# A two-layer decoder on one core: ternary weight passes moved to ScalarE, 63 expert blocks, the fourth convolution tile without diagonal products

## The reference

```
# layer 0, third block: top-4 of 32 experts
topk_logits, topk_idx = jax.lax.top_k(logits, K)
y = jnp.sum(outs * topk_weight[..., None], axis=1)      # outs: one row per token and chosen expert
# layer 1, first block: a state-space model
xz = jnp.einsum('bld,ed->ble', xn, in_proj_w)
x_inner, z = jnp.split(xz, 2, axis=-1)                  # 512 channels each
xc = conv_general_dilated(xc, conv_w, padding=[(3, 0)], feature_group_count=512) + conv_b
xc = silu(xc)
x_ssm = einsum('bld,ed->ble', xc, x_proj_w)             # 33 rows: B, C (16 states each) and dt
dt = softplus(x_ssm[..., -1:] * dt_w[:, 0] + dt_b)
h = dA * h + (dt_t * u_t) * B_t ;  y_t = sum(h * C_t) + D * u_t      # scan over 128 steps
# layer 1, third block, once for each of its two weight matrices
scale = 1.0 / clip(mean(abs(w)), EPS)
wq = clip(round(w * scale), -1, 1) / scale
```

## Time and profile before

| | us |
|---|---|
| median of three runs | 904.55 (903.81 to 906.38) |
| the profiled execution | 906.09 |
| its span | 904.3 |
| PE busy | 732.1 (81%) |
| DVE busy | 718.4 (79%) |
| ACT busy | 541.4 (60%) |
| POOL busy | 521.5 (58%) |

### The profile page before, as it was taken

How to read it: one execution, slowest core, us unless ns; L and a number is a source line. 1 busy time by engine, 2 the same in 40 slices (tenths; PEclk the granted TensorE clock), 3 DMA queues, 4 the chain that set the end, 5 groups by cost and what they waited for, 6 DMA issues and landing times. The chain is left out here.

```text
span 904.3 us, 14551 instructions
## 1 busy us (share of the span) xinstructions
PE 732.1 (81%) x4298; PEld 525.2 (58%) x4301; DVE 718.4 (79%) x1533; ACT 541.4 (60%) x1377; POOL 521.5 (58%) x542
## 2 busy tenths in 40 slices
PE   5899999999999884499999149959999999940365
PEld 3578888888888762377777124345555555630232
DVE  6667788888898875677777578497999999679886
ACT  2545565555556552466666525778998788037195
POOL 2057777777777861355553576627888799422211
PEclk8899999999999997599999559969999999975586
DMA  8726000000000500365546230032223222100000
...
DMA packets 29932, 70.80 MB, mean 78 GB/s; under 512 B 5440, under 2 KB 19584, under 8 KB 27552
## 3 DMA queue, kind: packets, MB, share of 16 engines
...
...
## 5 line engine op out<-in xcount | busy, mean ns | idle before, releaser
L1857 POOL TENSOR_TENSOR arena<-arena 128x1024 f32<-128x1024 f32 x63 | 148.4, 2382 | 45.7 <-DVE arena L1779 45.7
L1779 DVE TENSOR_TENSOR_SCAN arena<-arena,ps 128x1024 f32<-128x1024 f32 x64 | 143.7, 2277 | 12.6 <-PE ps L1504 7.3
L1525 PE MATMUL ps<-arena 128*128 128x512 f32 x256 | 120.1, 592 | 0.0
L645 PE MATMUL ps<-arena 128*128 128x128 f32 (+1 forms) x768 | 101.1, 282 | 0.9 <-PEq L373 0.9
L1086 POOL DMA_INDIRECT arena<-tokens,arena x64 | 62.6, 979 | 67.4 <-PE ps L1114 50.5
L645 PEld LDWEIGHTS ps<-arena 128*128 128x128 f32 (+1 forms) x768 | 91.6, 193 | 14.1 <-issue 12.9
L850 ACT ACTIVATE arena<-arena 128x128 f32<-128x128 f32 x256 | 98.8, 389 | 1.2 <-DVE arena L774 1.1
L858 ACT ACTIVATE arena<-ps 128x512 f32<-128x512 f32 x64 | 38.2, 597 | 86.6 <-PE ps L664 86.6
L1652 ACT ACTIVATE arena<-arena 128x1016 f32<-128x1016 f32 x64 | 72.3, 1135 | 19.1 <-DVE arena L1779 19.1
L1667 ACT ACTIVATE arena<-arena 128x256 f32<-128x256 f32 x192 | 81.3, 494 | 0.1
L905 POOL TENSOR_TENSOR arena<-arena 128x512 f32<-128x512 f32 x64 | 66.6, 1041 | 22.3 <-DVE arena L780 22.3
...
## 6 DMA issues: line engine op xcount, KB each, us to landing
...
```

Source lines behind the costliest of these rows:

```text
L645: t = eng.matmul(ps[:, i % 2, j * P:(j + 1) * P], L["wq"][0:L["kc"], c, GH * g + j, :], src[0:L["kc"], c, b * P:(b + 1) * P], start=c == 0 ...
L1525: t = eng.matmul(ps[:, 2 * k + r, :], ident, half(hC[s % 4], r), start=False, stop=n == ST - 1)
L1779: eng.tensor_tensor_scan(hst[s % 4], dA[s % 4], psD[s % 2].rearrange("p k m -> p (k m)"), 0.0, ALU.mult, ALU.add).then_inc(h_ready, 1)
L1857: eng.tensor_tensor(hC[s % 4], hst[s % 4], Csb[i % 4], ALU.mult).then_inc(hC_ready, 1)
```

## The change

- `RUNS` = (8*128*4 + 32*127) // 128 = 8160 // 128 = 63 takes the place of `NBLK` = 64 in the loops over groups and in the size of `expert_out`. It is the largest number of groups that any routing can give. The sizes of the index tables stay.
- `ternary` runs on ScalarE, between the diagonals and the first square root: four activations in place of three passes, each waiting for the one before. Its offsets come from four small memsets on VectorE. The inverse mean stays on VectorE and has a semaphore for ScalarE.
- `conv_diag`, `diagW` and their waits are gone. The fourth tile takes the way of the other three. VectorE's order is changed: `combine(5)` stands ahead of `conv(0, 0)`, the convolutions lie between the combines that are left, and `conv(3, 0)` and `conv(3, 1)` are new.
- `magnitudes` is gone. `steps` on VectorE writes v from PSUM, waits for it, and clears its sign bit into `dtu`; `exponentials` waits for each tile instead of for all four.

```diff
@@ -26,6 +26,7 @@
+RUNS = (NB * P * TOPK + E * (P - 1)) // P
...
         hd = nc.dram_tensor("tokens", (T, D), fp32).ap()
-        ys = nc.dram_tensor("expert_out", (NBLK * P, D), fp32).ap()
...
             def _(eng):
-                for s in range(NBLK):
+                for s in range(RUNS):
...
+                    eng.wait_ge(y_out[u], 16 * ((RUNS + 3 - u) // 4))
...
                         turn(s + 2)
-                    if s + 1 < NBLK:
+                    if s + 1 < RUNS:
                         gate_up(s + 1)
                     if s >= 1:
                         down(s - 1)
-                    if s < NBLK:
...
+        offsets = view(o + 6, 4)
+        offsets_in, wsc_ready = sem("ternary_offsets"), sem("ternary_scale")
+        wcl_ready = sem("ternary_mean")
@@ -1311,9 +1315,12 @@
         def ternary(eng, ch, k, w, wq):
-            ch.link(eng.tensor_scalar(w, w, wsc[:, k:k + 1], MAGIC, ALU.mult, ALU.add))
-            ch.link(eng.tensor_scalar(w, w, -MAGIC, -1.0, ALU.add, ALU.max))
-            ch.link(eng.tensor_scalar(wq, w, 1.0, None, ALU.min))
+            eng.wait_ge(offsets_in, 4)
+            eng.wait_ge(wsc_ready, 1)
+            ch.link(eng.activation(w, w, ACT.Identity, scale=wsc[:, k:k + 1], bias=offsets[:, 0:1]))
+            ch.link(eng.activation(w, w, ACT.Relu, scale=-1.0, bias=offsets[:, 1:2]))
+            ch.link(eng.activation(w, w, ACT.Relu, scale=-1.0, bias=offsets[:, 2:3]))
+            ch.link(eng.activation(wq, w, ACT.Identity, bias=offsets[:, 3:4]))
...
-        diagW = view(room[8], 512, "p (k m) -> p k m", k=KCONV)
...
-        DIAG_BANK, PROJ_BANK = (0, 5), (4, 7)
-        XC_ORDER = ((0, 3, 1, 2), (0, 1, 2, 3))
+        PROJ_BANK = (4, 7)
...
-                def conv_diag(k):
-                    for j in range(KCONV):
-                        t = eng.matmul(ps[:, DIAG_BANK[k], :].rearrange(tq, b=HB), diagW[:, j],
-                                       padded[CT - 1][:, k * HB:(k + 1) * HB, j:j + P], start=j == 0, stop=j == KCONV - 1)
-                    t.then_inc(diag_done, 1)
-
                 def bc_dt(k):
-                    for n, c in enumerate(XC_ORDER[k]):
-                        eng.wait_ge(xc_ready, CT * k + n + 1)
+                    for c in range(CT):
+                        eng.wait_ge(xc_ready, CT * k + c + 1)
                         t = eng.matmul(ps[0:3 * E + 1, PROJ_BANK[k], :], w_bc[:, c, :], half(xc[:, c], k),
-                                       start=n == 0, stop=n == CT - 1)
+                                       start=c == 0, stop=c == CT - 1)
                     t.then_inc(proj_done, 1)
...
                     project(CT + m, Z_BANK[0][m], 0).then_inc(z_done, 1)
-                eng.wait_ge(diag_in, KCONV)
-                eng.wait_ge(pad_ready, CT)
-                eng.wait_ge(xi_ready, CT)
-                conv_diag(0)
-
                 eng.wait_ge(z_ready, CT)
                 normS.pe(eng, tiles=HALVES[1])
                 eng.wait_ge(normS.hT_ready, 4)
...
                     project(m, XI_BANK[1][m], 1).then_inc(xi_done, 1)
                 bc_dt(0)
                 dt_rows(0)
-                eng.wait_ge(xi_ready, 2 * CT)
-                conv_diag(1)
                 bc_dt(1)
                 dt_rows(1)
                 for m in range(CT):
...
-                w0 = KCONV * (CT - 1)
-                for j in range(KCONV):
-                    eng.activation(diagW[:, j], ident, ACT.Copy, scale=cw[:, w0 + j:w0 + j + 1]).then_inc(diag_in, 1)
                 for c in range(CT):
                     eng.activation(diagD[:, c], ident, ACT.Copy, scale=Dp[:, c:c + 1]).then_inc(diag_in, 1)
...
                 def xi(n, k):
                     m = n
                     eng.wait_ge(xi_done, CT * k + n + 1)
-                    if m < CT - 1:
-                        last = KCONV * m + KCONV - 1
-                        eng.activation(half(xc[:, m], k), ps[:, XI_BANK[k][m], :], ACT.Identity, bias=cb[:, m:m + 1],
-                                       scale=cw[:, last:last + 1])
+                    last = KCONV * m + KCONV - 1
+                    eng.activation(half(xc[:, m], k), ps[:, XI_BANK[k][m], :], ACT.Identity, bias=cb[:, m:m + 1],
+                                   scale=cw[:, last:last + 1])
                     eng.activation(padded[m][:, k * HB:(k + 1) * HB, PAD:], ps[:, XI_BANK[k][m], :].rearrange(tq, b=HB),
                                    ACT.Copy).then_inc(xi_ready, 1)
                 def conv_silu(n, k):
-                    c = XC_ORDER[k][n]
-                    if c < CT - 1:
-                        eng.wait_ge(conv_ready, (CT - 1) * k + c + 1)
-                        eng.activation(half(xc[:, c], k), half(xc[:, c], k), ACT.Silu).then_inc(xc_ready, 1)
-                    else:
-                        eng.wait_ge(diag_done, k + 1)
-                        eng.activation(half(xc[:, c], k), ps[:, DIAG_BANK[k], :], ACT.Silu,
-                                       bias=cb[:, c:c + 1]).then_inc(xc_ready, 1)
+                    eng.wait_ge(conv_ready, CT * k + n + 1)
+                    eng.activation(half(xc[:, n], k), half(xc[:, n], k), ACT.Silu).then_inc(xc_ready, 1)
                 def bc_rows(k):
                     eng.wait_ge(proj_done, k + 1)
                     eng.activation(half(bcf[0:3 * E + 1], k), ps[0:3 * E + 1, PROJ_BANK[k], :],
                                    ACT.Copy).then_inc(bcf_ready, 1)
-                def magnitudes(k):
-                    eng.wait_ge(dt_done, k + 1)
+                def exponentials(k):
                     for c in range(CT):
-                        eng.activation(half(dtu[:, c], k), ps[:, k, :], ACT.Abs, bias=dtb[:, c:c + 1],
-                                       scale=dtw[:, c:c + 1]).then_inc(abs_ready, 1)
-
-                def exponentials(k):
-                    eng.wait_ge(abs_ready, CT * (k + 1))
-                    for c in range(CT):
+                        eng.wait_ge(abs_ready, CT * k + c + 1)
                         eng.activation(half(dtu[:, c], k), half(dtu[:, c], k), ACT.Exp, scale=-1.0).then_inc(exp_ready, 1)
+                tw = Chain(eng, s_wq)
+                ternary(eng, tw, 0, w1, w1q)
+                ternary(eng, tw, 1, w2, w2q)
                 scales_root(eng, 0)
                 normS.act(eng, nw, pairs=(0, 2))
...
                 conv_silu(0, 1)
                 conv_silu(1, 1)
                 bc_rows(0)
-                magnitudes(0)
                 conv_silu(2, 1)
                 conv_silu(3, 1)
                 exponentials(0)
                 eng.activation(negA, negA, ACT.Exp).then_inc(s_negA, 1)
                 bc_rows(1)
-                magnitudes(1)
                 exponentials(1)
                 eng.wait_ge(exp_ready, 2 * CT)
                 for c in range(CT):
...
-                ch, cw_, cs = Chain(eng, s_comb), Chain(eng, s_wq), Chain(eng, s_scale)
+                ch, cs = Chain(eng, s_comb), Chain(eng, s_scale)
...
                 def steps(k):
-                    eng.wait_ge(abs_ready, CT * (k + 1))
+                    eng.wait_ge(dt_done, k + 1)
                     for c in range(CT):
                         eng.tensor_scalar(half(dts[:, c], k), ps[:, k, :], dtw[:, c:c + 1],
                                           dtb[:, c:c + 1], ALU.mult, ALU.add).then_inc(zz_ready, 1)
+                        eng.wait_ge(zz_ready, CT * k + c + 1)
+                        eng.tensor_scalar(half(dtu[:, c], k).bitcast(u32), half(dts[:, c], k).bitcast(u32), 0x7FFFFFFF, None,
+                                          ALU.bitwise_and).then_inc(abs_ready, 1)
...
+                for k, value in enumerate((MAGIC, MAGIC + 1.0, 2.0, -1.0)):
+                    eng.memset(offsets[:, k:k + 1], value).then_inc(offsets_in, 1)
...
                 ch.wait()
                 eng.wait_ge(wsum_done, 1)
-                cw_.link(eng.tensor_scalar(wcl, ps[:, 3, 300:302], 1.0 / (D * INNER), 1e-5, ALU.mult, ALU.max))
-                cw_.link(eng.reciprocal(wsc, wcl))
-                ternary(eng, cw_, 0, w1, w1q)
-                combine(0)
-                ternary(eng, cw_, 1, w2, w2q)
-                for b in range(1, HB):
+                eng.tensor_scalar(wcl, ps[:, 3, 300:302], 1.0 / (D * INNER), 1e-5, ALU.mult, ALU.max).then_inc(wcl_ready, 1)
+                eng.wait_ge(wcl_ready, 1)
+                eng.reciprocal(wsc, wcl).then_inc(wsc_ready, 1)
+                for b in range(HB):
                     combine(b)
                 normS.dve_variance(eng, 0)
                 scales_in(eng, cs, 0)
                 scales_out(eng, cs, 0)
                 combine(HB)
+                combine(HB + 1)
                 conv(0, 0)
-                for b in range(HB + 1, NB):
-                    combine(b)
+                combine(HB + 2)
+                conv(1, 0)
+                combine(HB + 3)
                 normS.dve_variance(eng, 1)
                 scales_in(eng, cs, 1)
-                conv(1, 0)
```

(5 more changed lines are left out.)

27 lines of the change are left out of this document (14 added, 13 removed).

## The result

The changed kernel takes 908.89 us (median of 6 runs, 906.53 to 909.97) against 904.52 (903.49 to 907.33) of the kernel before beside it: a ratio of 1.0052, with a 95% interval of 1.0031 to 1.0073. It is 4.4 us slower, where 901.6 and a gain were forecast. The profiled execution took 908.29, its span is 906.6.

The account below looks back on a forecast made before the run. No engine bounds the whole; behind the expert loop, alternating chains of engines set the time. 1.8 us for the group plus 1.1 us up to the scan make 2.9 off 904.55: 901.65, rounded to 901.6, range 898.5 to 903.6.

Parts of the forecast that it names:

- 63 groups: Expert loop: one turn less, with its gather, products and write, saves 1.8 us (bounds 1.6 to 2.0).
- Ternary passes on ScalarE: Ahead of the first root: 16.4 us of passes fill ScalarE's idle time, so the root comes 1.75 us earlier.
- Rivals B and D: Behind the loop: ScalarE's chain ends late, 902.8, or only the group saves, 902.7; chance 0.22 together.
- VectorE's new order: First half's convolutions and combines: second half's `h` comes 2.95 us earlier, 1.2 more than the root gave.
- The sum: Whole kernel: 1.8 us from the group and 1.1 us up to the scan, 2.9 us saved in all.
- The gap on TensorE: Second half's projections start at 1.2 GHz without the diagonal products, costing 1.96 us; convolutions come 1.0 us earlier than before.
- Rival A: Second half's projections: the clock holds despite the 2.7 us gap, saving 5.7 us in all, 898.9; chance 0.20.
- Fourth convolution, v and |v|: Second half on VectorE: fourth tile adds 2.3 us, v and sign 5.0 plus 1.0 contention; `bc_rows(1)` 1.25 us earlier.
- rival C: Second half: sign passes wait for GpSimd's `split`, four costing 8.2 us instead of 1.0; 908.8, chance 0.05.
- To the scan: From `dt_rows(1)` through the z projections: 0.15 us given back, `dt_and_dtu` 1.1 us earlier (bounds 0 to 4.0).
- The range: Whole kernel, 8 in 10: 898.5 to 903.6 us; faster 0.54, same 0.40, slower 0.06.

Follow-up runs that it names:

- after_light: Changed kernel with half of the expert gathers left out, each gathered row used twice; 900.67 us, ratio 0.9965 to the kernel before.
- the filler: Changed kernel with four GpSimd memsets holding gathers back, plus TensorE products nobody reads where the diagonal products were; 903.69 us, ratio 0.9998 to the kernel before.
- sign_only: Kernel before with only the sign change: VectorE makes |v| out of v instead of ScalarE out of PSUM; 903.68 us, ratio 1.0001.
- the brake: Four GpSimd memsets of about 1 us behind four gathers; 905.53 us on the changed kernel, 904.12 on the kernel before with only ternary passes moved.
- ternary_paced: Kernel before with only the ternary passes moved to ScalarE, plus four GpSimd memsets of about 1 us behind four gathers; 904.12 us, ratio 1.0002.
- ternary_only: Kernel before with only the ternary passes moved to ScalarE; 908.32 us, ratio 1.0043 to the kernel before.

## Why the prediction was wrong, point by point

**63 groups: right.** 63 copies, 381.0 to 492.4, 1.80 us each. The kernels put the group at 2.3, 1.25 and 0.3 us, and at 1.9 when it is undone: in agreement with 1.8, without fixing it.

**Ternary passes on ScalarE: right in every duration.** 2.10 and 2.00 us a pass and 16.4 us for both matrices, as forecast; sum to root 22.84 us, which is 1.66 earlier for 1.75. Rivals B and D, in which the root gains nothing, are out. The Trainium skill, "ScalarE: Activation LUTs", "Rules for kernel authors", would keep this work off ScalarE; on the price the trace agrees with it (2.00 against 1.28 us), and the root came earlier all the same. "Four gathers, all beside those passes, make up most of it; I take 3.7": the gathers' steps became 3.84 us shorter. Right as well, and the closer gathers are what made the signals later.

**VectorE's new order: wrong, the step that failed.** "The first convolution waits for `xi`: 540.29 - 1.75 = 538.54, and one combine more is done ahead of it." I had shifted every row behind the root by 1.75 us and taken that a finished product is heard of at once, as in the one trace that I had. Measured on pieces, root to second `h` became 28.66 us for 22.1: +6.6 us, all the loss and more. The late signals explain it: ScalarE's second `xi` came 9.4 us after its product, and VectorE waited up to 1.65 us between its own steps. `after_light`, with half the gathers, has the 21.94 us that the arithmetic had asked for, so the durations were right, and the missing term was the price of denser gathers on the signals of TensorE and VectorE. The sum held it at nothing. The new order added to it, since it put the second convolution, and with it a late signal, ahead of `h`. The faster gathers of the step before were booked as pure gain. I had looked at what they cost from the side of GpSimd alone, and at who waits for them, not at what they do to others while they run.

**The gap on TensorE: right.** The granted clock is 0.50 as the second half's projections begin, they take 8.56 us, and their first `xi` comes 3.45 us behind (forecast: 3.5). The gap was 9.33 us and not 2.7, since late signals came on top, but the granted clock shows only the two levels, 0.50 and 1.00. Rival A is out by this; the filler's 2.17 us for 1.96 show that the mechanism was priced right.

**Fourth convolution, v and |v|: right.** `h` to `bc_rows(1)` took 24.73 and 25.06 us in the two traces of the changed kernel, for 24.9. Twelve convolution steps of the second half took 10.83 us for 10.0. The four pairs of v and |v| took from 570.63 to 575.78, 5.15 us for the 6 that I had allowed:

```profile
570.63 0.80 DVE L1693 TENSOR_SCALAR arena<-ps,arena 128x512 f32<-128x512 f32 x1
571.47 0.66 DVE L1696 TENSOR_SCALAR arena<-arena 128x512 uint32<-128x512 uint32 x1
...
575.35 0.43 DVE L1696 TENSOR_SCALAR arena<-arena 128x512 uint32<-128x512 uint32 x1
```

A sign pass is 0.43 us alone and here 0.66 at most beside GpSimd's `split`; in four other traces (`sign_only` is one) the longest took 1.22 or 1.23, still far below what rival C needs. So rival C, the one slower case that I had, priced at 908.8, is out although the time came out at 908.9: its 8.2 us would have to stand in these rows. That the forecast's slower case had nearly the right time is chance.

**To the scan: half wrong.** Forecast 11.65, measured 13.83 and 12.43. Behind an idle time of 4.58 us the two short instructions of `dt_rows(1)` took 2.07 us for 1.12, and the z projections 10.21, with the granted clock at 0.50 up to 585, where I gave 0.15 back on 8.83. In the second trace the z projections took 8.82. In the kernel before, the same piece is 11.50 in one trace and 10.22 in another, the z projections alone 8.83 us in the one and 7.13 in the other. I treated as fixed what varies by 1.3 us from execution to execution.

**The range.** It left out any loss larger than the contention of rival C, at 5%. The bounds were made of durations; none was made of waits that the trace of before doesn't show. A second trace of the kernel before would have shown a wait of 4.96 us for work already done.

**Open.** The traces show increments recorded late and engines that wait for them; they don't show what holds them. The number of gathers, rows or small packets matters and not the bytes, and the delay outlasts the last packet by 3 us when the gathers are dense. In that stretch there is no packet of instruction loading (the changed kernel's last is at 525.99), so it isn't missing instructions. The records themselves thin out in the same order. Of the 512 increments that the 32 gathers make, 512 are recorded in the trace of before, which alone has no late signal; 210 to 272 in the ten traces in which VectorE's passes or the brake slow the gathers; and 89 to 101 in the five dense ones. But in `after_light`, where nothing is late, it is 95 of 256, so thin records by themselves don't make signals late. The waits went through, so the increments came; what is missing is their record. Recording them may still be a part of the delay, and no run here is known to be free of it. Whether the issuing, the small packets, the recording or another path that all share holds the signals wasn't told apart. That `ternary_paced` takes 4.2 us less than `ternary_only` in the medians while signals are still late in its trace isn't explained in full.
